# Output projection of a gated recurrence as plain fp32 matmuls on h·y and w_out, in place of three reduced-precision products on high and low parts

## What is computed

```python
# recurrent branch (L = 256 channels)
y    = gelu(xn @ w_y + b_y)
conv = conv_b + sum_k conv_w[k] * shifted(xn @ w_x + b_x)      # 4 taps
gate_x, gate_a = sigmoid(conv @ w_ig + b_ig), sigmoid(conv @ w_ag + b_ag)
log_a = -8 * gate_a * softplus(a_param)
a, mult = exp(log_a), sqrt(1 - exp(2 * log_a))                 # token 0: a = 0, mult = 1
h_t  = a_t * h_{t-1} + gate_x * conv * mult                    # scan over 512 tokens
attn = (h * y) @ w_out + b_out
# feed-forward branch (682 hidden units), w1, w3, w2 quantised to {-1, 0, 1} times a scale
ffn  = (silu(xn @ w1q.T) * (xn @ w3q.T)) @ w2q.T
out  = x + attn + ffn
```

## Time and profile before

| | us |
|---|---|
| median of 3 runs | 89.52 |
| lowest and highest run | 88.8, 89.9 |
| profiled execution: span from first to last instruction | 87.7 |

### The profile page before, as it was taken

How to read it: one execution, slowest core, us unless ns; L and a number is a source line. 1 busy time by engine, 2 the same in 40 slices (tenths; PEclk the granted TensorE clock), 3 DMA queues, 4 the chain that set the end, 5 groups by cost and what they waited for, 6 DMA issues and landing times.

```text
span 87.7 us, 1098 instructions
## 1 busy us (share of the span) xinstructions
PE 72.9 (83%) x376; PEld 61.9 (71%) x376; DVE 73.9 (84%) x107; ACT 51.8 (59%) x80; POOL 54.4 (62%) x47
## 2 busy tenths in 40 slices
PE   5991999999999999649799999999999830199950
PEld 5980798988878877418476888879999820199840
DVE  0189987599999999999999665999999929999970
ACT  4643799696999994505394987978966020202200
POOL 7205500050965199998099997699999999490000
PEclk9999759999999999999999999999999999555999
DMA  1999999300000000000000000000000000000085
GB/s 17 303 288 332 342 358 366 110 7 0 0 4 0 0 0 0 0 0 0 0 4 0 0 7 0 0 0 0 0 0 0 0 0 0 0 7 0 0 271 207
DMA packets 5141, 5.75 MB, mean 66 GB/s; under 512 B 444, under 2 KB 4624, under 8 KB 5136
## 3 DMA queue, kind: packets, MB, share of 16 engines
q1 hardware_dynamic: 4992, 5.68, 19.4%
q10 hardware_dynamic: 144, 0.01, 0.2%
HBM read 4.64 MB, written 1.05 MB: 65 GB/s over the span
## 4 chain that ended last, share of the span: by engine, by line
DVE 38%; PE 26%; POOL 17%; issue 10%; DMA 4%; ACT 2%; DVEq 1%; POOLq 0%
DVE conv L524 17%; POOL x_sb L236 13%; PE slot L663 8%; PE slot L680 7%; DVE tx L574 5%; PE slot L761 5%; DVE w_raw L551 5%; DMA x_sb<-x 4%; PE slot L722 3%; DVE tx L576 3%; POOL g_lo L246 2%; PE slot L652 2%; DVE xn_y L472 2%; DVE stats L447 2%; POOL tx L269 1%
## 5 line engine op out<-in xcount | busy, mean ns | idle before, releaser
L246 POOL TENSOR_TENSOR g_lo<-w_raw,g_hi 128x512 fp32r<-128x512 f32 x10 | 17.1, 1727 | 3.7 <-ACT g_hi L357 3.0
L680 PE MATMUL slot<-xt_hi,w_q 128*128 128x512 f32 x40 | 16.0, 401 | 0.8 <-DVE w_raw L551 0.7
L680 PE MATMUL slot<-xt_lo,w_q 128*128 128x512 f32 x40 | 15.7, 394 | 0.0
L524 DVE SCALAR_TENSOR_TENSOR conv<-xb,par,conv 128x512 f32<-128x512 f32 x12 | 15.3, 1327 | 0.0
L236 POOL TENSOR_TENSOR x_sb<-x_sb,b_out_bc 128x256 f32<-128x256 f32 x8 | 11.8, 1509 | 0.0
L221 POOL TENSOR_TENSOR w_lo<-w_raw,w_hi 128x512 fp32r<-128x512 f32 x5 | 6.9, 1382 | 7.0 <-ACT w_hi L282 7.0
L722 PE MATMUL slot<-w_hi,conv_hi 128*128 128x256 f32 x16 | 5.6, 364 | 5.9 <-ACT conv_hi L395 5.8
L680 PEld LDWEIGHTS slot<-xt_hi,w_q 128*128 128x128 f32 x40 | 7.5, 188 | 3.7 <-DVE w_raw L551 2.1
L228 POOL TENSOR_SCALAR conv<-xb,par 128x512 f32<-128x512 f32 x4 | 3.9, 982 | 9.9 <-ACT xb L330 9.9
L357 ACT ACTIVATE g_hi<-w_raw 128x512 fp32r<-128x512 f32 x8 | 5.0, 628 | 8.2 <-DVE w_raw L551 8.2
L710 PE MATMUL slot<-w_q,g_hi 128*128 128x256 f32 x40 | 9.5, 281 | 0.0
(11 more groups left out here) (113 smaller groups left out, 188.6 us busy)
## 6 DMA issues: line engine op xcount, KB each, us to landing
w_raw<-w13t SPq DMA_DIRECT2D x2, 682.0 KB, 8.1
w_raw<-dense SPq DMA_DIRECT2D x5, 256.0 KB, 7.7
out<-x_sb SPq DMA_DIRECT2D x3, 256.0 KB, 2.2
w_raw<-w2t SPq DMA_DIRECT2D x1, 640.0 KB
x_sb<-x SPq DMA_DIRECT2D x2, 256.0 KB, 3.3
x_sb<-x SPq DMA_DIRECT2D x1, 512.0 KB, 5.7
out<-x_sb SPq DMA_DIRECT2D x2, 128.0 KB, 2.1
b_out_bc<-b_out SPq DMA_DIRECT2D x1, 128.0 KB, 7.1
```

Source lines behind the costliest of these rows:

```text
L246: nc.gpsimd.tensor_tensor(g_lo[:, j, s], g[:, n % RING], g_hi[:, j, s].bitcast(f32), ALU.subtract).then_inc(g_lo_set, 1)
L524: nc.vector.scalar_tensor_tensor(out=conv[:, s, c], in0=xb[:, s, c, k:k + SEQ], scalar=par[:, CONV_W + KC * k + c:CONV_W + KC * k + c + 1] ...
L680: mm = nc.tensor.matmul(slot[H_SLOT[s][j]][:, o], w13_q[:, c, col:col + P], v[:, s, c], start=(c == 0 and v is xt_hi), stop=(c == KC - 1 a ...
```

## The change

The output projection takes h·y as it is (`tx`) and w_out as loaded (`w_raw[:, WOUT]`), both plain float32: one matmul per tile and chunk in place of three. High and low parts of both are gone: `square_hi(WOUT)` on ScalarE, `square_lo(WOUT)` on POOL, the four copies of h·y on ScalarE, and its low parts, two on POOL and two on DVE. Since WOUT's raw weights must now live to the end, the tail's silu moves to the memory of `below`, and its activation waits for w2 to be quantised in place of the split of WOUT. `project(s)` now runs chunk 0 over all tiles and banks and then chunk 1.

```diff
--- before.py
+++ after.py
@@ -104,7 +104,7 @@
 
         w_flat = w_raw[:, :, :, :].rearrange("p m c n -> p (m c n)")
         silu = w_flat[:, 0:RING * SEQ].rearrange("p (r n) -> p r n", r=RING)
-        silu_t = w_flat[:, RING * SEQ:RING * SEQ + TOKENS]
+        silu_t = below[:, :, :].rearrange("p c n -> p (c n)").bitcast(f32)[:, 0:TOKENS]
         w13_flat = w13_raw[:, :, :].rearrange("p c n -> p (c n)")
         g = w13_flat[:, 0:RING * SEQ].rearrange("p (r n) -> p r n", r=RING)
         g_t = w13_flat[:, RING * SEQ:RING * SEQ + TOKENS]
@@ -161,7 +161,6 @@
         a_set, a2_set, mult_set, mult0_set = sem("a_set"), sem("a2_set"), sem("mult_set"), sem("mult0_set")
         nx_last_set = sem("nx_last_set")
         nx_step, nx_set, h_set, hy_set = sem("nx_step"), sem("nx_set"), sem("h_set"), sem("hy_set")
-        hy_hi_set, hy_lo_set = sem("hy_hi_set"), sem("hy_lo_set")
         h_psum, silu_set, g_set, g_hi_set, g_lo_set = (
             sem("h_psum"), sem("silu_set"), sem("g_set"), sem("g_hi_set"), sem("g_lo_set"))
         t_psum, silu_t_set, g_t_set, gt_hi_set, gt_lo_set = (
@@ -253,7 +252,6 @@
             square_lo(WIG)
             square_lo(WAG)
             lo_of_conv(0)
-            square_lo(WOUT)
             for n in range(6):
                 lo_of_g(n)
             lo_of_conv(1)
@@ -267,10 +265,6 @@
                 pool.wait_ge(nx_step, s + 1)
                 pool.wait_ge(mult_set, KC * (s + 1))
                 nc.gpsimd.tensor_tensor(tx[:, s, 1], tx[:, s, 1], xb[:, s, 1, TAPS - 1:], ALU.mult).then_inc(nx_last_set, 1)
-            for c in range(KC):
-
-                pool.wait_ge(hy_hi_set, c + 1)
-                nc.gpsimd.tensor_tensor(conv_lo[:, 0, c], tx[:, 0, c], conv_hi[:, 0, c].bitcast(f32), ALU.subtract).then_inc(hy_lo_set, 1)
 
 
         @block.scalar
@@ -390,10 +384,6 @@
                 for c in range(KC):
                     nc.scalar.activation(xb[:, s, c, TAPS:], xb[:, s, c, TAPS:], ACT.Sqrt, scale=-0.25, bias=quarter[:, 0:1]).then_inc(mult_set, 1)
 
-            def hy_hi_of(s, c):
-                act.wait_ge(hy_set, KC * s + c + 1)
-                nc.scalar.activation(conv_hi[:, s, c], tx[:, s, c], ACT.Copy).then_inc(hy_hi_set, 1)
-
             square_hi(WIG)
             gelu_of(0)
             gelu_of(1)
@@ -404,7 +394,6 @@
             conv_hi_of(0)
             silu_of(2)
             g_hi_of(0)
-            square_hi(WOUT)
             g_hi_of(1)
             silu_of(3)
             g_hi_of(2)
@@ -419,7 +408,7 @@
             g_hi_of(6)
             gate_a(0)
             act.wait_ge(t_psum, 1)
-            act.wait_ge(w_lo_set, WOUT + 1)
+            act.wait_ge(w2_q_set, 1)
             nc.scalar.activation(silu_t[HALF:HALF + TAIL], slot[TAIL_SLOT][0:TAIL].rearrange("p s n -> p (s n)"), ACT.Silu,
                                  scale=scale[0:TAIL, 0:1]).then_inc(silu_t_set, 1)
             silu_of(7)
@@ -432,9 +421,6 @@
             decays(1)
             mult_of(0)
             mult_of(1)
-            for s in range(SEQS):
-                for c in range(KC):
-                    hy_hi_of(s, c)
 
 
         @block.vector
@@ -574,11 +560,6 @@
                     nc.vector.tensor_tensor_scan(tx[:, s, c], ta[:, s, c], tx[:, s, c], 0.0, ALU.mult, ALU.add).then_inc(h_set, 1)
                     dve.wait_ge(h_set, KC * s + c + 1)
                     nc.vector.tensor_tensor(tx[:, s, c], tx[:, s, c], y[:, s, c], ALU.mult).then_inc(hy_set, 1)
-
-            def lo_of_second_hy(c):
-                dve.wait_ge(hy_lo_set, KC)
-                dve.wait_ge(hy_hi_set, KC + c + 1)
-                nc.vector.tensor_tensor(conv_lo[:, 1, c], tx[:, 1, c], conv_hi[:, 1, c].bitcast(f32), ALU.subtract).then_inc(hy_lo_set, 1)
 
             def output(n):
 
@@ -635,10 +616,7 @@
             squares(1)
             recurrence(0)
             recurrence(1)
-            lo_of_second_hy(0)
-            output(0)
-            lo_of_second_hy(1)
-            for n in range(1, len(O_ALL)):
+            for n in range(len(O_ALL)):
                 output(n)
 
 
@@ -712,31 +690,15 @@
 
             def project(s):
 
-                pe.wait_ge(w_lo_set, WOUT + 1)
-
-                def terms(i, ready, operands):
-                    for c in range(KC):
-                        pe.wait_ge(ready, KC * s + c + 1)
-                        for t in O_TILES[s][i]:
-                            for v, w in operands:
-                                mm = nc.tensor.matmul(out_tile(s, i, t), v[:, s, c, t * P:(t + 1) * P], w[:, WOUT, c], start=False,
-                                                      stop=(v is conv_lo and c == KC - 1), skip_group_check=True)
-                    return mm
-
-                def hi_terms(i):
-                    terms(i, hy_hi_set, [(conv_hi, w_hi), (conv_hi, w_lo)])
-
-                def lo_terms(i):
-                    terms(i, hy_lo_set, [(conv_lo, w_hi)]).then_inc(o_psum, 1)
-
-
-                banks = len(O_TILES[s])
-                hi_terms(0)
-                for i in range(1, banks):
-                    hi_terms(i)
-                    lo_terms(i - 1)
-                lo_terms(banks - 1)
-
+                pe.wait_ge(w_loaded[WOUT], 16)
+                for c in range(KC):
+                    pe.wait_ge(hy_set, KC * s + c + 1)
+                    for i, tiles in enumerate(O_TILES[s]):
+                        for t in tiles:
+                            mm = nc.tensor.matmul(out_tile(s, i, t), tx[:, s, c, t * P:(t + 1) * P], w_raw[:, WOUT, c], start=False,
+                                                  stop=(c == KC - 1), skip_group_check=True)
+                        if c == KC - 1:
+                            mm.then_inc(o_psum, 1)
 
 
             pe.wait_ge(ones_set, 1)
```

## The result

| | before | changed |
|---|---|---|
| median, us | 89.48 | 85.98 (84.54 to 86.64, 4 runs) |
| ratio, 95% interval | | 0.952 [0.943, 0.961] |
| profiled span, us | 87.7 | 83.5 |

The medians are of all runs; the ratio is of the faster runs alone, as some executions of either kernel fall into a slower state (here 86.38 and 86.64 of the changed one). The profiled execution of the changed kernel took 85.58 us as a whole, 2.1 more than its span (1.8 was assumed). The prediction said 85.5, and 83.7 for the span.

A forecast was written before the change was run, and what follows sets the result against it. No engine bounds throughout; after 71.87 a serial tail, its first 9.3 us DVE's. Span 87.7 - 3.66 (tail) - 0.7 (WOUT's split) + 0.35 (clock) = 83.7, with 1.8 around it 85.5 us; range 84.4 to 88.1.

The forecast's parts named there:

- POOL's low parts of h·y slow DVE: DVE's tail after 71.87: without POOL's two low parts the last h·y ends 2.3 us earlier, bounds 0 and 2.8.
- half of that stretch counts as lost: DVE's scan at 71.87, beside POOL's second input product for 1.2 us: taken as 1.7 us, bounds 1.21 and 2.27.
- The copies: PE's last group waits for DVE's product instead of ScalarE's copy of h·y: 0.7 us more gained.
- can start at 78.87: PE's last projection group, one sequence and half the contraction, starts at 78.87 instead of 81.88, waiting for DVE's product.
- A plain matmul at 0.44 (upper bound): PE's projection: two passes of 0.218 at full clock per matmul, 1.74 per group of four; lower end 0.94 per group.
- The end behind the last h·y: After 78.87, the first bank is complete at 79.9, the last three output additions take 1.46 and end at 81.4.
- The clock: PE's gap from 71.9 to 74.35: a clock fall there ends the additions 0.7 later; half, 0.35, was taken.
- rival A: Projection: the clock stays down as long as before, returning 5 us after work resumes, at 79.4; 86.6 us, chance 0.18.
- WOUT's split: At 32 us: without POOL's low part (1.75) DVE's taps have less company; 0.7 us gained, bounds 0 and 1.75.
- The waiting semaphore of the tail's activation: The activation at 49.93 waits for w2 to be quantised, which ends at 47.43: 2.5 us of slack, no cost.
- Rival B: DVE is slow in the tail whoever runs beside it: 1.4 us gained, nothing at 32 us, 88.1 us, chance 0.12.
- rival C: PE becomes the bound, at half clock from 74.35 to the end, PE ending at 84.9; 90.0 us, chance 0.05.

The follow-up runs named there:

- the two profiles that had it up: The changed kernel run again (median 85.80, ratio 0.968), and the changed kernel with 12 plain matmuls filling PE's gap in the projection (85.33, 0.951).
- the changed kernel's second profile: The changed kernel measured once more, with nothing altered: median 85.80 us, span 84.4, ratio 0.968 to the kernel before.
- the two POOL experiments: Changed kernel plus two POOL subtractions beside the recurrence: 87.90 us, 0.990. Kernel before without POOL's two low parts of h·y and their eight matmuls: 88.73, 0.989.
- the two late profiles: The changed kernel run again (first tap 24.98, ratio 0.968), and the changed kernel with ScalarE's four copies of h·y put back (first tap 25.50, ratio 0.975).

## Why the prediction was right, point by point

- **POOL's low parts of h·y slow DVE: right in mechanism, 1.78 measured for 2.3 predicted** (in the traces; the runs without the low parts gained less). The term that was mis-sized is the first scan, "half of that stretch counts as lost", 1.7. It took 2.27 in every kernel in which POOL's second product was issued just ahead of it (70.22 for the scan at 70.29). Exclusion explains the number: POOL ends at 71.47, and a free scan of 1.21 begun then would end at 72.68; it ended at 72.56. There is no half: the DVE instruction waits for nearly the whole one in flight.
- **The copies: 0.7 predicted, 0.66 by the later start of PE in the run with them put back** (0.8 with what the clock added there). But the step as I put it, the last group "can start at 78.87", waiting for h·y alone, held only where the clock stayed up. In the first profile PE was behind, and the group began 0.6 after its h·y.
- **A plain matmul at 0.44 (upper bound): right.** Passes start 0.215 us apart at full clock and 0.43 at half. The lower bound of 0.118 is out, and the Trainium skill's four passes (FP8 and Floating Point Precision, TensorE Precision Notes), an estimate of 0.43 us, agree: 0.43 measured. PE's growth was indeed hidden in gaps.
- **The end behind the last h·y: 2.57 predicted with the clock up, 2.57 and 2.58 measured** in the two profiles that had it up. The path is the predicted one: in the changed kernel's second profile the last group starts at 79.08, its first bank is complete at 80.10 and the last three additions start at 80.14. DVE's other two additions end at 80.11, so with a faster group they would hold the end, as predicted.
- **The clock: half of 0.7 taken for not knowing; 0.47 when it falls.** The two profiles show 0.47 and nothing, so the 0.35 is near neither but by averaging. It did fall in the first profile and not in the second, after the same gap of 2.6 us. So my wish to decide from the gap's length could not be met. It was back by 76.5, 3.2 us after work had resumed, and not 5, so rival A did not come.
- **WOUT's split: 0.7 predicted, 1.41 measured at g of block 6, 1.19 passed on.** The term was mis-sized by stopping at one tap: with POOL 1.7 us ahead, both last taps are free, one wholly (1.05) and one by the rest of an instruction (0.36). Past that PE became the bound: in the chain after, 5.86 us of gate products from 39.13, the tail block and hidden blocks 7 to 9 follow each other without a wait for DVE, where before DVE led until 47.35. That gives 0.22 back.
- **The waiting semaphore of the tail's activation: nothing, as predicted.** Quantising ended at 45.6 and the activation started at 48.14.
- **Rival B** (DVE is slow whoever runs beside it) falls with the two POOL experiments: with POOL's work added the product with y takes 1.57, with it taken away 0.69, and ScalarE's copies are there in the second and not in the first; **rival C** with the passes at 0.215: PE ended at 80.3, not 84.9.
- The total, 4.0 predicted in the span and 4.2 measured, is closer than its terms, by luck: the tail gave 0.7 less, the stretch before 48 us 0.5 more after what PE took back, and 0.39 came from the front, which the change does not touch.

## What to carry to other kernels

Before moving an elementwise instruction to POOL because POOL is free, ask what DVE runs at that moment: if DVE's instructions read two SBUF tensors and are on the path, POOL's instruction costs DVE nearly its full time (0.88 of 1.05 here), and it can be cheaper to do the work on DVE itself (0.69 us). Splitting an operand for a faster product also pays for the split, in copies before PE and low parts beside DVE. Where PE waits for its operand anyway, a product of fewer, slower matmuls on the raw operand is the shorter path, as long as the gaps hold its growth.

## What the runs showed of the hardware that I had not expected

- POOL and DVE exclude each other for whole instructions. A POOL subtraction of 512 columns issued beside DVE ends 1.05 to 1.13 us after the DVE instruction in flight; a DVE product alone is 0.69 and behind a POOL instruction 1.57, a tap 0.74 and 1.79, a scan 1.22 and 2.10 to 2.27. DVE products with their second input in PSUM were untouched (0.73 for a product for g, beside POOL or not). Two SBUF inputs are not the only case: with one SBUF input a cast took 1.12 us beside POOL's additions and 0.69 where they had been moved away, and the comparison above 2.70 and 1.79.
- Plain fp32 warm-ups raise the clock too: in the changed kernel's profile the same 24 passes took 4.75 us instead of 5.49, with the last ones at full pace. In these records a clock row of 1.00 ahead of the first change is no measurement: the warm-ups have the durations of half clock there.
- The first tap varies by 2.8 us between profiles, and the clock's fall in the first 15 us is one part of it. It starts at 22.67 and 22.87 where the clock stayed up (with 16 warm-ups, and once with 12; 23.27 with additions moved in front of it); with about 3.4 us at half clock at 23.89 to 24.98; with twice that at 24.30 and 25.50. Four more warm-up matmuls over PE's idle time kept it up in the two profiles that had them.
- The second part is the same exclusion, by timing. In the two late profiles (24.98 and 25.50) a DVE instruction on 128x4 elements, 0.17 us in the changed kernel's first profile, took 0.94 and 0.86: it came at 10.35 and 10.70, into a POOL low part that ended at 11.26 and 11.53, and ended 0.03 after it. That this delay alone moved the first tap is not shown.
